# Attention and a gated feed-forward on one core: the second half of a pair's value product in three bursts instead of two

## The chip, the cores and the metric

The kernel runs on one NeuronCore of a Trainium2 chip. The metric is the device time of one execution in microseconds (us), as the median of several runs; lower is better. Engines are named as in the profile: PE (TensorE matmul), PEld (its weight loads), DVE (VectorE), ACT (ScalarE), POOL (GpSimd), and SP, which here only issues DMAs. Every engine takes its own instructions in the order in which they are written.

## What is computed

Input x is 4 batches of 1024 tokens with 128 channels. The reference, cut to what matters:

```
q, k, v = einsum('bsx,xMnd->Mbnsd', x, qkv)             # 16 heads of 64
a = q k^T * 64**-0.5 + bias                             # bias: cumulative by distance, -30000 above the diagonal
mix = softmax(a) v
x = layernorm(x + einsum('bnsd,ndx->bsx', mix, out_w))
xr, xk = blends of x and x shifted by one token         # by mu_r, mu_k
out = sigmoid(xr W_r) * (square(relu(xk W_k)) W_v)
x = layernorm(x + out)
```

## The kernel before, in words

The work goes in 32 pair steps, n = 0 to 31: 4 batches times 8 pairs of heads (`drive`, line 225). A pair has 16 rows of 128 queries; row r belongs to one head h and one query tile i (`ROWS`, line 26). Rows 0 to 7 are the query tiles 0 to 3 of both heads and rows 8 to 15 the tiles 4 to 7. A row of query tile i covers i + 1 key tiles (causal), so rows 0 to 7 are 1, 2, 3, 4, 1, 2, 3, 4 key tiles wide, and rows 8 to 15 are 5, 6, 7, 8, 5, 6, 7, 8.

A pair step has 16 slots, and every engine has its own loop over the slots (`step` on lines 343, 514, 704 and 998). What happens to a row runs across the engines: PE computes its scores four slots ahead (`score`, line 900; `LEAD` = 4), DVE adds the bias and takes the row's minimum (`bias`, line 605), ACT takes exp and the sum (`exps`, line 458), DVE takes the reciprocal of the sum (`invert`, line 620, issued one slot later, behind the next row's `bias`), POOL multiplies the row by it (`normalise`, line 406), PE transposes the row in slot r (`transpose`, line 921) into one of two PSUM banks in turn, four key tiles to a bank, and ACT or DVE copies each bank to SBUF (`evacuate`, lines 466 and 624; which engine, by the string `EVACUATOR`, line 63). A bank of `transpose` waits for the copy two banks earlier. In the text T(r) is the transpose of row r, S(r) its scores; S(16) is row 0 of the next pair. With the banks of rows 7, 8 and 9 it goes so: row 7 is one bank, copied by ACT; row 8 is two, the first copied by DVE and the second by ACT; row 9 is two, both by DVE. So T(9) waits for DVE's copy of row 8's first bank.

The transposed rows times v are the pair's mix (`mix`, line 934): for each key tile j and both heads one matmul, summed in the PSUM bank `ps_o`. The near half (g = 0, query tiles 0 to 3, key tiles 0 to 3) is done in slot 11 of the same step (`MIX_NEAR`). The far half (g = 1, query tiles 4 to 7, key tiles 0 to 7) can only start when row 15's transposes are copied, so it is done in the next step, in two bursts of four key tiles, in slots 2 and 5 (`MIX_FAR`, line 83; PE's `step`, lines 1006 to 1008). Key tiles 0 to 4 take 512 columns, 5 to 7 take 384, 256 and 128. Within a slot PE's order is: scores, projection chunk, tile step, far mix, near mix, transposes (lines 999 to 1011). When the last key tile is done, DVE copies `ps_o` to `mix_sb` (`store_mix`, line 635), the far half at the end of slot `MIX_FAR[1] + 1` = 6, the near half in slot 12.

Slots 2, 3, 5, 7, 10 and 14 also hold the six projection chunks of the next pair (`PROJ_SLOTS`, line 73; `project`, line 873): chunks 0 and 1 are q, 2 and 3 are k, 4 and 5 are v, all through the one PSUM bank `ps_m`. A q or k chunk is rounded by ACT (`q_hi`, `k_hi`, line 450) and its rest is taken by DVE (`q_lo`, `k_lo`, line 601); the next user of `ps_m` waits for that (`wait_chunk`, line 855). From step 9 on a step also carries one tile of 128 tokens of the feed-forward (`tile_step`, lines 951, 640 and 478), whose matmuls use `ps_m` too: the output projection in slot 0 (line 960), the transpose of the normalised tile X1 in slot 4 (line 965), two products in slot 9 and one in slot 12. Steps 1 to 8 have far bursts but no tile; step 31 has a tile but no chunks.

SP issues the DMAs in one order (lines 343 to 377): the tables and weights to come, after chunk 1 the four pieces of `stacks` from q, then `store_mix(n - 1, 1)` (line 363; it waits for DVE's copy of the far half), then after chunk 3 the eight pieces of `stacks` from k (line 279), then `x_res` and `mix_tile` for the next step's tile (lines 325 and 329), then `store_mix(n, 0)`. S(16) waits for the stacks of head 0, the output projection for `mix_tile`.

Of the kernel before, what the change touches and what calls it, by code (L numbers as in the profile page):

```python
# [15 lines left out]
GROUP = 4  # L16
# [49 lines left out]
def evacuated(engine, k):  # L66

    return sum(int(c) == engine for c in EVACUATOR[:k + 1])
# [11 lines left out]
V_PROJ, LN2_RSTD, LN2 = 12, 13, 13  # L80
TILE_MATMULS = (OUT_PROJ, X1_T, RK_PROJ, V_PROJ)
WIDE = 4
MIX_FAR = (2, 5)
MIX_NEAR = 11
TILE_LAG = PAIRS + 1
CH = 13
# [2 lines left out]
def build(nc, x, qkv, out_w, rpe, w_r, w_k, w_v, mu_r, mu_k, out):  # L89
# [13 lines left out]
    with ExitStack() as ctx:  # L103
# [149 lines left out]
        def rows_ahead(n, more, slot):  # L253

            if slot + LEAD < NROWS:
                return [(n, slot + LEAD)]
            return [(n + 1, slot + LEAD - NROWS)] if more else []
# [317 lines left out]
        def _(dve):  # L575
# [19 lines left out]
            def project(m, c):  # L595

                dve.wait_ge(s_hi, 4 * m + c + 1)
                which, at = chunk_of(m, c)
                hi, lo, scale = ((q_hi, q_lo, SCALE), (k_hi, k_lo, 1.0))[which]
                half = slice(512 * at, 512 * at + 512)  # L600
                nc.vector.scalar_tensor_tensor(out=lo[:, half], in0=proj_bank(m, c), scalar=scale,  # L601
                                               in1=hi[:, half].bitcast(F32), op0=ALU.mult, op1=ALU.subtract)\
                    .then_inc(s_lo, 1)

            def bias(n, r):

                h, i = ROWS[r]
                width = P * (i + 1)
                if i % GROUP == 0:
                    dve.wait_ge(s_table[n % 2][h], 16 * (n // 2) + 16)  # L610

                before = (r - PSLOTS) % NROWS
                dve.wait_ge(s_tr, NBANKS * (n if before > r else n + 1) + sum(b[0] <= before for b in BANKS))
                dve.wait_ge(s_score, NROWS * n + r + 1)
                nc.vector.tensor_tensor_reduce(prob[:, r % PSLOTS, 0:width],  # L615
                                               ps_rows[:, score_at(r):score_at(r) + width],
                                               table[n % 2][:, h, 0:width][:, ::-1], 1.0, 3.0e38, ALU.add, ALU.min,
                                               low[:, r:r + 1]).then_inc(s_biased, 1)

            def invert(n, r):  # L620
                dve.wait_ge(s_exp, NROWS * n + r + 1)
                nc.vector.reciprocal(inv[:, r:r + 1], total[:, r:r + 1]).then_inc(s_inv, 1)  # L622

            def evacuate(n, k):
                r, b0, nb = BANKS[k]
                h, i = ROWS[r]
                g = i // GROUP
                dve.wait_ge(s_pv, 2 * n + g + 1)
                if n == 0 and r == 3 * GROUP:
                    dve.wait_ge(s_xt_dram, 16 * (BATCH - 1))  # L630
                dve.wait_ge(s_tr, NBANKS * (n + 1) + k + 1)
                nc.vector.tensor_copy(pt[h][g][:, b0:b0 + nb, P * (i % GROUP):P * (i % GROUP) + P],  # L632
                                      ps_t[k % 2][:, 0:nb * P].rearrange("p (b s) -> p b s", s=P)).then_inc(s_ev[0], 1)

            def store_mix(n, g):
                dve.wait_ge(s_pv, 2 * n + g + 3)
                dve.wait_ge(s_mix_d[g], 16 * n + 16)
                nc.vector.tensor_copy(mix_sb[g][:, :], ps_o[:, :]).then_inc(s_o, 1)  # L638
# [65 lines left out]
            def step(n, prev, tile_too, more):  # L704
                for slot in range(NROWS):
                    for row in rows_ahead(n, more, slot):
                        bias(*row)
                    for row in rows_ahead(n, more, slot - 1):
                        invert(*row)
                    if more and slot in PROJ_SLOTS[:4]:  # L710
                        project(n + 1, PROJ_SLOTS.index(slot))
                    for k in range(NBANKS):
                        if BANKS[k][0] == slot and EVACUATOR[k] == "0":
                            evacuate(n, k)
                    if prev and slot == MIX_FAR[1] + 1:
                        store_mix(n - 1, 1)
                    if slot == MIX_NEAR + 1:
                        store_mix(n, 0)
                    if tile_too:
                        tile_step(n, slot)  # L720

            drive(step)

            def add_residual(w):
# [101 lines left out]
        def _(pe):  # L826
# [73 lines left out]
            def score(n, r):  # L900

                h, i = ROWS[r]
                if n == 0 and r == 0:
                    pe.wait_ge(s_first, 96)
                elif i % GROUP == 0:
                    pe.wait_ge(s_stack[h], 96 * n + 96)

                pe.wait_ge(s_biased, NROWS * n + r + 3 - rows_since(r))
                at, width = score_at(r), P * (i + 1)
                cut = BANK - at % BANK  # L910
                for c0, c1 in ((0, min(cut, width)), (cut, width)):
                    if c0 >= c1:
                        continue
                    c1 = max(c1, c0 + SHORTEST)
                    for low_part in range(2):
                        ins = nc.tensor.matmul(ps_rows[:, at + c0:at + c1], q_st(h, n)[:, P * i:P * i + P],  # L916
                                               k_st(h, n, low_part)[:, c0:c1], start=(low_part == 0),
                                               stop=(low_part == 1))
                ins.then_inc(s_score, 1)

            def transpose(n, r):
                pe.wait_ge(s_norm, NROWS * n + r + 1)
                for k in (k for k in range(NBANKS) if BANKS[k][0] == r):
                    _, b0, nb = BANKS[k]

                    engine = int(EVACUATOR[k - 2])
                    pe.wait_ge(s_ev[engine], EVACUATED[engine] * (n + (k >= 2)) + evacuated(engine, (k - 2) % NBANKS))
                    for b in range(nb):
                        at = P * (b0 + b)
                        ins = nc.tensor.transpose(ps_t[k % 2][:, P * b:P * b + P], prob[:, r % PSLOTS, at:at + P],  # L930
                                                  ident[:, :])
                    ins.then_inc(s_tr, 1)

            def mix(n, g, first, end):

                if first == 0:
                    pe.wait_ge(s_v, 2 * n + 2)
                    for which in range(2):
                        last_bank = max(k for k in range(NBANKS) if ROWS[BANKS[k][0]][1] < GROUP * (g + 1))
                        pe.wait_ge(s_ev[which], EVACUATED[which] * (n + 1) + evacuated(which, last_bank))  # L940
                    pe.wait_ge(s_o, 2 * n + g + 1)
                final = GROUP * (g + 1) - 1
                for j in range(first, end):
                    c0 = P * max(0, j - GROUP * g)
                    for h in range(2):
                        ins = nc.tensor.matmul(ps_o[D * h:D * h + D, c0:], v_pair[n % 2][:, j, D * h:D * h + D],  # L946
                                               pt[h][g][:, j, c0:], start=(j == 0), stop=(j == final))
                    if j == final:
                        ins.then_inc(s_pv, 1)
# [48 lines left out]
            def step(n, prev, tile_too, more):  # L998
                for slot in range(NROWS):
                    for row in rows_ahead(n, more, slot):  # L1000
                        score(*row)
                    if more and slot in PROJ_SLOTS:
                        project(n + 1, PROJ_SLOTS.index(slot), tile_too)
                    if tile_too:
                        tile_step(n, slot, more)
                    if prev and slot in MIX_FAR:
                        at = GROUP * MIX_FAR.index(slot)
                        mix(n - 1, 1, at, at + GROUP)
                    if slot == MIX_NEAR:
                        mix(n, 0, 0, GROUP)  # L1010
                    transpose(n, slot)

            drive(step)

            def out_project(w):
# [81 lines left out]
```

## Time and profile before

| what | value |
|---|---|
| median of 3 runs | 1245.46 us (1243.80, 1245.46, 1245.80) |
| the profiled execution's own time | 1246.39 us |
| its span, first to last instruction | 1244.6 us |
| mean granted TensorE clock | 0.988 of full speed |
| PE busy | 1118.1 us, 90% |
| POOL busy | 886.9 us, 71% |
| DVE busy | 843.3 us, 68% |
| ACT busy | 743.1 us, 60% |
| chain that ended last | PE 65%, DVE 17%, issue 8%, ACT 6% |

Busy shares are means over all stages. A row of a timeline is: start in us from the span's start, length, engine, line, operation, written tile <- read tiles, shape, number of instructions run together, and in brackets the engine's idle time before it and what ended that. The length of a PE row runs to a modelled end, so the distance between the starts of neighbours is the better measure of what a PE instruction costs. A matmul on fp32 data shows as two rows.

### The profile page before, as it was taken

What the parts mean: (1) busy time and instruction counts of PE and PEld (TensorE: products, weight loads), DVE (VectorE), ACT (ScalarE), POOL (GpSimd) and SP (SyncE); (2) the same over time, 40 slices, a digit from 0 to 9 for tenths busy, and PEclk for the clock granted to TensorE, in tenths of its full rate; (3) what the DMA queues carried; (4) which work ended last, traced back from release to release, by engine and by line L of the source; (5) the groups of instructions that cost most, each with busy time, mean ns of one, the idle gap of its engine ahead of it and who ended that gap; (6) DMA issues with size and microseconds to landing.
All of it is one profiled execution on the core that took longest, in us unless ns stands there. A gap on an engine that the chain in (4) does not pass through costs nothing.

```text
span 1244.6 us, 21976 instructions
## 1 busy us (share of the span) xinstructions
PE 1118.1 (90%) x6909; PEld 781.9 (63%) x6909; DVE 843.3 (68%) x2505; ACT 743.1 (60%) x1857; POOL 886.9 (71%) x527
## 2 busy tenths in 40 slices
PE   5899999999999999999999999999999999999885
PEld 3666666666666666666666666666666666666664
DVE  2666666666676767777667777666777676777746
ACT  3666666666655656656665656665656566656623
POOL 1877777878876677876677876677876677776730
PEclk9899999999999999999999999999999999999997
DMA  8855445555655455655465654456654455654600
GB/s 199 208 122 124 115 117 122 130 132 134 157 138 115 116 141 127 160 137 129 116 141 132 159 127 118 117 140 153 159 123 115 123 134 142 155 122 110 213 18 20
DMA packets 101745, 163.69 MB, mean 132 GB/s; under 512 B 10592, under 2 KB 66288, under 8 KB 101632
## 3 DMA queue, kind: packets, MB, share of 16 engines
q1 hardware_dynamic: 99472, 161.37, 53.4%
q10 hardware_dynamic: 2160, 0.92, 0.3%
q8 instruction: 58, 0.95, 0.3%
q14 instruction: 55, 0.45, 0.1%
HBM read 41.63 MB, written 19.96 MB: 49 GB/s over the span
## 4 chain that ended last, share of the span: by engine, by line
PE 65%; DVE 17%; issue 8%; ACT 6%; POOL 2%; DMA 1%; DVEq 0%; SPq 0%; ACTq 0%
PE ps_o L946 21%; PE ps_t L930 15%; PE ps_rows L916 13%; PE ps_m L891 7%; DVE prob L615 4%; DVE pt L632 4%; PE ps_m L960 4%; PE ps_m L896 3%; ACT pt L474 2%; DVE mix_sb L638 2%; POOL prob L410 2%; ACT prob L463 1%; DVE k_lo L601 1%; DVE q_lo L601 1%; DVE shift L682 1%
## 5 line engine op out<-in xcount | busy, mean ns | idle before, releaser
L410 POOL TENSOR_SCALAR prob<-prob,inv 128x128 f32<-128x128 f32 (+7 forms) x512 | 880.5, 1730 | 308.2 <-DVE inv L622 306.2
L463 ACT ACTIVATE prob<-prob,low 128x128 f32<-128x128 f32 (+7 forms) x512 | 395.3, 773 | 119.1 <-DVE low L615 116.9
L615 DVE CUSTOM_DVE_ANT_0 prob<-ps_rows,table 128x128 f32<-128x128 f32 (+7 forms) x512 | 383.6, 749 | 72.7 <-PE ps_rows L916 66.2
L930 PE MATMUL ps_t<-ident,prob 128*128 128x128 f32 x2304 | 349.1, 278 | 87.2 <-ACT pt L474 50.1
L916 PE MATMUL ps_rows<-stacks 128*128 128x512 f32 (+3 forms) x1536 | 402.5, 372 | 4.6 <-DVE w_t L700 3.2
L930 PEld LDWEIGHTS ps_t<-ident,prob 128*128 128x128 f32 x2304 | 260.6, 141 | 198.3 <-issue 130.6
L632 DVE COPY pt<-ps_t 128x256 f32<-128x256 f32 (+2 forms) x320 | 179.1, 568 | 179.6 <-PE ps_t L930 178.8
L474 ACT ACTIVATE pt<-ps_t 128x128 f32<-128x128 f32 (+2 forms) x448 | 203.6, 477 | 110.8 <-PE ps_t L930 110.6
L946 PE MATMUL ps_o<-pt,v_pair 128*64 128x512 f32 (+3 forms) x1536 | 268.7, 492 | 0.0
L916 PEld LDWEIGHTS ps_rows<-stacks 128*128 128x128 f32 x1536 | 246.3, 191 | 22.7 <-DVE w_t L700 3.4
L946 PEld LDWEIGHTS ps_o<-pt,v_pair 128*64 128x64 f32 x1536 | 101.8, 136 | 181.8 <-issue 172.3
L891 PE MATMUL ps_m<-x_cur,w_cur 128*128 128x512 f32 x250 | 130.6, 604 | 0.0
L622 DVE RECIPROCAL inv<-total 128x1 f32<-128x1 f32 x512 | 81.7, 160 | 71.6 <-ACT prob L463 70.0
L450 ACT ACTIVATE q_hi<-ps_m 128x512 fp32r<-128x512 f32 x63 | 37.2, 590 | 119.4 <-PE ps_m L891 119.4
L463 ACT ACTIVATION_READ_ACCUMULATOR prob<-prob,low 128x1 f32 x512 | 98.0, 191 | 0.0
L896 PE MATMUL ps_m<-w_cur,x_cur 128*128 128x128 f32 x504 | 66.4, 275 | 0.0
L896 PEld LDWEIGHTS ps_m<-w_cur,x_cur 128*128 128x128 f32 x504 | 65.1, 191 | 0.1
L601 DVE SCALAR_TENSOR_TENSOR q_lo<-ps_m,q_hi 128x512 fp32r<-128x512 f32 x63 | 43.6, 692 | 26.7 <-ACT q_hi L450 26.6
L455 ACT ACTIVATE v_pair<-ps_m 128x512 f32<-128x512 f32 x63 | 37.6, 597 | 28.1 <-PE ps_m L896 27.6
L484 ACT ACTIVATE lnv<-mv,eps 128x1 f32<-128x1 f32 x48 | 14.1, 295 | 65.3 <-DVE mv L653 36.9
L891 PEld LDWEIGHTS ps_m<-x_cur,w_cur 128*128 128x128 f32 x250 | 43.3, 191 | 11.7 <-issue 5.8
L960 PE MATMUL ps_m<-wo,mix_tile 128*128 128x128 f32 x384 | 47.8, 279 | 0.0
(108 smaller groups left out, 561.6 us busy)
## 6 DMA issues: line engine op xcount, KB each, us to landing
stacks<-k_hi SPq DMA_DIRECT2D x126, 256.0 KB, 4.7
stacks<-k_lo SPq DMA_DIRECT2D x126, 256.0 KB, 4.9
stacks<-q_hi SPq DMA_DIRECT2D x63, 256.0 KB, 3.7
stacks<-q_lo SPq DMA_DIRECT2D x63, 256.0 KB, 4.4
mix_transposed<-mix_sb SPq DMA_DIRECT2D x62, 256.0 KB, 2.0
table<-bias_by_distance SPq DMA_DIRECT2D x64, 192.0 KB, 3.7
mix_tile<-mix_transposed SPq DMA_DIRECT2D x24, 512.0 KB, 5.0
w_cur<-in_L_attn_qkv SPq DMA_DIRECT2D x31, 192.0 KB, 3.9
```

The source lines that it names most:

```text
L410: nc.gpsimd.tensor_scalar(row, row, inv[:, r:r + 1], None, ALU.mult).then_inc(s_norm, 1)
L463: nc.scalar.activation(row, row, ACT.Exp, bias=low[:, r:r + 1], scale=-1.0, accum_out=total[:, r:r + 1]).then_inc(s_exp, 1)
L474: nc.scalar.activation(pt[h][g][:, b0:b0 + nb, P * (i % GROUP):P * (i % GROUP) + P], ps_t[k % 2][:, 0:nb * P].rearrange("p (b s) -> p b s" ...
L615: nc.vector.tensor_tensor_reduce(prob[:, r % PSLOTS, 0:width], ps_rows[:, score_at(r):score_at(r) + width], table[n % 2][:, h, 0:width][:, ...
L622: nc.vector.reciprocal(inv[:, r:r + 1], total[:, r:r + 1]).then_inc(s_inv, 1)
L632: nc.vector.tensor_copy(pt[h][g][:, b0:b0 + nb, P * (i % GROUP):P * (i % GROUP) + P], ps_t[k % 2][:, 0:nb * P].rearrange("p (b s) -> p b s ...
L891: ins = nc.tensor.matmul(proj_bank(m, c), w_cur[m % 2][:, which, :], x_cur[:, 512 * at:512 * at + 512], start=True, stop=True)
L896: ins = nc.tensor.matmul(proj_bank(m, c)[:, P * t:P * t + P], x_cur[:, at:at + P], w_cur[m % 2][:, 2, :], start=True, stop=True)
L916: ins = nc.tensor.matmul(ps_rows[:, at + c0:at + c1], q_st(h, n)[:, P * i:P * i + P], k_st(h, n, low_part)[:, c0:c1], start=(low_part == 0 ...
L930: ins = nc.tensor.transpose(ps_t[k % 2][:, P * b:P * b + P], prob[:, r % PSLOTS, at:at + P], ident[:, :])
L946: ins = nc.tensor.matmul(ps_o[D * h:D * h + D, c0:], v_pair[n % 2][:, j, D * h:D * h + D], pt[h][g][:, j, c0:], start=(j == 0), stop=(j == ...
L960: ins = nc.tensor.matmul(ps_m[:, 0:C], mix_tile[:, p, :], wo[:, p, :], start=(p == 0), stop=(p == PAIRS - 1))
```

## The change

The far half is cut in three bursts in place of two: key tiles 0 and 1 in slot 1, 2 and 3 in slot 4, 4 to 7 in slot 7. DVE's copy of the finished half, and with it SP's store, moves from slot 6 to slot 8. No instruction is added or taken away.

```
-MIX_FAR = (2, 5)
+MIX_FAR = {1: (0, 2), 4: (2, 4), 7: (4, 8)}
...
-                    if prev and slot == MIX_FAR[1] + 1:
+                    if prev and slot == max(MIX_FAR) + 1:
                         store_mix(n - 1, 1)
...
                     if prev and slot in MIX_FAR:
-                        at = GROUP * MIX_FAR.index(slot)
-                        mix(n - 1, 1, at, at + GROUP)
+                        mix(n - 1, 1, *MIX_FAR[slot])
```

## Rows read from the trace of the kernel before

**Rows 1.** Busy time in one step with a tile: stretch, length, PE, PEld, DVE, ...

```profile
636.60:674.10 37.50, 34.48 (x216) 24.14 (x216) 26.72 (x81) 23.10 (x60) 27.61 (x17) 1.00 0.55 132
```

**Rows 2.** Timeline of PE, first half of that step, slots 2 to 9

```profile
640.56 1.10 PE L891 MATMUL ps_m<-x_cur,w_cur 128*128 128x512 f32 x2
641.59 3.65 PE L946 MATMUL ps_o<-pt,v_pair 128*64 128x512 f32 x16
645.17 0.55 PE L930 MATMUL ps_t<-ident,prob 128*128 128x128 f32 x3
...
646.03 1.02 PE L891 MATMUL ps_m<-x_cur,w_cur 128*128 128x512 f32 x2
...
648.46 0.33 PE L965 MATMUL ps_m<-ident,x 128*128 128x128 f32 x1 [0.39 <-DVE q_lo L601]
...
649.44 1.02 PE L891 MATMUL ps_m<-x_cur,w_cur 128*128 128x512 f32 x2
650.39 2.37 PE L946 MATMUL ps_o<-pt,v_pair 128*64 128x512 f32 x16
...
655.05 1.02 PE L891 MATMUL ps_m<-x_cur,w_cur 128*128 128x512 f32 x2
655.91 0.60 PE L930 MATMUL ps_t<-ident,prob 128*128 128x128 f32 x4
...
659.70 0.85 PE L930 MATMUL ps_t<-ident,prob 128*128 128x128 f32 x6 [0.76 <-DVE pt L632]
```

**Rows 3.** Timeline of DVE, same step, slots 6 to 9

```profile
655.65 0.68 DVE L638 COPY mix_sb<-ps_o 128x512 f32<-128x512 f32 x1
...
658.86 0.69 DVE L632 COPY pt<-ps_t 128x512 f32<-128x512 f32 x1
...
660.43 1.02 DVE L632 COPY pt<-ps_t 128x512 f32<-128x512 f32 x2
```

**Rows 4.** Timeline of PE, a step without a tile: T(7) and T(9)

```profile
216.37 0.60 PE L930 MATMUL ps_t<-ident,prob 128*128 128x128 f32 x4
...
220.16 0.85 PE L930 MATMUL ps_t<-ident,prob 128*128 128x128 f32 x6 [1.21 <-DVE pt L632]
```

**Rows 5.** Timeline of PE, second half of the first step, to the next step's slot 0

```profile
662.10 0.93 PE L930 MATMUL ps_t<-ident,prob 128*128 128x128 f32 x7
...
666.19 1.09 PE L930 MATMUL ps_t<-ident,prob 128*128 128x128 f32 x8
667.04 0.49 PE L916 MATMUL ps_rows<-stacks 128*128 128x256 f32 x2
...
669.73 0.85 PE L930 MATMUL ps_t<-ident,prob 128*128 128x128 f32 x6 [0.97 <-ACT pt L474]
...
672.51 0.96 PE L930 MATMUL ps_t<-ident,prob 128*128 128x128 f32 x7 [0.69 <-ACT pt L474]
...
675.23 0.94 PE L960 MATMUL ps_m<-wo,mix_tile 128*128 128x128 f32 x7
```

**Rows 6.** Timeline of DVE, same step: the reciprocal of row 15

```profile
669.13 0.16 DVE L622 RECIPROCAL inv<-total 128x1 f32<-128x1 f32 x1 [0.48 <-ACT prob L463]
```

**Rows 7.** Timeline of SP's DMA issues, same step

```profile
656.36 0.33 SPq L320 DMA_DIRECT2D mix_transposed<-mix_sb  x1
658.16 1.10 SPq L279 DMA_DIRECT2D stacks<-k_hi  x2
...
667.84 0.99 SPq L329 DMA_DIRECT2D mix_tile<-mix_transposed  x1
```

**Rows 8.** Line 279, 659.7 to 660.9 us: the two k_lo pieces of head 0

```profile
L279 SPq DMA_DIRECT2D stacks<-k_lo x2: 647/990/1333, 659.3 to 660.0; - x2
...
DMA to landing us min/median/max: 4.5/4.9/5.3
```

**Rows 9.** Line 329, all 24 loads of mix_tile, issue to landing

```profile
DMA to landing us min/median/max: 4.7/5.0/5.6
```

**Rows 10.** DMA traffic from 662 to 668 us

```profile
DMA packets 396, 1.31 MB, mean 219 GB/s; under 512 B 77, under 2 KB 77, under 8 KB 395
...
q1 hardware_dynamic: 395, 1.30, 100.2%
```

## Prediction

> **What bounds the kernel now.** I read the page's shares first (PE 90%), then one step by stretch, then PE's timeline of it, and only then the engines that PE waits for. In a step with a tile PE is busy for 34.48 of 37.5 us, POOL for 27.6, DVE for 26.7, ACT for 23.1, at a granted clock of 1.00 [rows 1]. So PE sets the step, and what can be won or lost is its idle time. The reader should look for the brackets. The timeline shows four: 0.39 us before X1 in slot 4, until DVE has q_lo of chunk 1; 0.76 before T(9), until DVE has copied row 8 [rows 2]; 0.97 before T(13) and 0.69 before T(14), both for ACT copies [rows 5]. A step without a tile has 1.21 before T(9) [rows 4]. The change touches what lies before the first two; the later ones only matter as room.
>
> The wait before T(9) is DVE's doing. DVE copies the far half at 655.65, 0.68 us long, ahead of the bias of rows 11 and 12, and so reaches row 8's copy at 658.86, although PE has finished T(7) near 656.5 [rows 2, 3].
>
> **What moves on PE.** No instruction is added, so PE's own work stays, but for the entry into a burst. A q or k chunk lasts 0.86 from start to next start ahead of transposes (655.05 to 655.91) and 1.03 or 0.95 ahead of a burst [rows 2]: an entry costs about 0.1 to 0.17. Two entries become three. I take +0.03 a step with a tile and +0.1 without, with 0 and 0.17 as ends.
>
> **Cover lost: chunk 0 to chunk 1.** Chunk 1 waits until ACT and DVE have read chunk 0 out of the one bank. The same wait with nothing long over it is chunk 1 to X1: 646.03 to 648.46, 2.43 us, 0.39 of it idle [rows 2]. Before, the burst of 3.58 us in slot 2 (641.59 to 645.17) hid it. Afterwards slot 2 has no burst. Between chunks 0 and 1 PE has the chunk (0.86) and T(2) with S(7) (645.17 to 646.03, 0.86), 1.72 us, so it idles 2.43 - 1.72 = 0.71 us, in every step with chunks. X1 keeps its 0.39, as the slot 4 burst is issued behind it. Chunk 2 also loses its burst, but between chunks 2 and 3 there are 655.05 - 649.44 = 5.61 us, less the burst's 2.30 and its entry 3.2, still above 2.43: nothing.
>
> **The wait before T(9) changes hands.** With the copy of the far half gone from slot 6 and PE's slots 5 and 6 free of a burst, DVE has row 11 biased early. But the last burst now lies in slot 7, ahead of T(7). ACT's copy of T(7) stands ahead of the exp of row 11 on ACT; DVE's reciprocal of row 11 waits for that exp and stands ahead of the copy of row 8; T(9) waits for that copy. The same sequence exists one half later: T(11) starts at 666.19, then ACT's copy, the exp of the 8-tile row 15, and the reciprocal starts at 669.13, 2.94 us [rows 5, 6]. T(7) is 0.49 shorter (0.60 against 1.09), so 2.45. Then some 0.1 to the copy, 0.69 for it, and 0.15 to PE (659.55 to 659.70) [rows 2, 3]: 3.38 us from the start of T(7) to T(9). PE's own work there is 659.70 - 0.76 - 655.91 = 3.03 with a tile and 220.16 - 1.21 - 216.37 = 2.58 without [rows 2, 4]. So it still idles 0.35 (before 0.76) or 0.80 (before 1.21): a gain of 0.41 in both.
>
> Balance of the first half: with a tile +0.71 - 0.41 + 0.03 = +0.33 us, without +0.71 - 0.41 + 0.1 = +0.40 us.
>
> **DVE behind it.** The copy of the far half (0.68) now follows row 8's copy and delays row 13's bias and the two copies for T(10). From 659.55 to 660.43 DVE needs 0.88, then 1.02 for both copies; with 0.33 of shift and 0.62 for the store they end near 662.4, the first near 662.0. T(10) comes at 662.10 + 0.33 = 662.43 and needs the second only four transposes later [rows 3, 5]. Cost nothing, with 0.2 to 0.3 to spare; if the cover is gone, up to 0.3. The near mix waits for the same copy, but only in slot 11. POOL has 10 us idle in the step [rows 1].
>
> **SP behind it.** The far store waits for the copy, and the eight k pieces, x_res and mix_tile are queued behind the store. T(9) is now near 660.03, the copy of row 8 ends 0.15 earlier, the far copy near 660.5; then the store's issue (0.33) and the k pieces near 660.85 in place of 658.16: the whole train is 2.7 us later [rows 2, 3, 7]. Two takers are behind it.
> - S(16): the fourth k piece is issued at 660.0 and lands 5.3 later, 665.3 [rows 8]; then at 668.0, and S(16) wants it at 667.04 + 0.33. PE waits some 0.7 there. But T(13) waits 0.97 for ACT and T(14) 0.69 [rows 5], which this eats: nothing, with 0.8 as the other end.
> - mix_tile: issued at 667.84, 5.0 to land, 672.84 [rows 7, 9]; then 675.55, and the output projection wants it at 675.23 + 0.33 = 675.56 [rows 5]. It just fails to be hidden. The store's 256 KB now go right ahead of the train, so I take 0.2 us, ends 0 and 0.8 (a landing of 5.6 [rows 9] and the store).
>
> The train drains at 219 GB/s with the queue 100% busy [rows 10], so a late start is a late end. The Trainium skill (DMA: Bandwidth & Descriptors, Where 436 GB/s comes from) says instead that copies between places in SBUF are bound by the fabric at 435 GB/s; by that, the train would make up the delay, mix_tile would cost nothing, and the sum would be the first rival's. The trace has half that rate for the very same copies, and the measurement decides.
>
> **Sum.** Steps 9 to 30: 22 x (0.33 + 0.2) = 11.7. Steps 1 to 8: 8 x 0.40 = 3.2. Step 31 has no chunks and so no new gap, and I count it as nothing, though it may win a little. Together +14.9 us on the profiled execution's 1246.39, or 1261.3; that execution is 0.93 above the median, so 1260.4 for the median. I say **1260**.
>
> **Rivals.**
> - The transfers are hidden after all: the store's 0.2 is absent, because the train drains faster than rows 10 or because S(16) moves the next step too. Then 22 x 0.33 + 3.2 = 10.5, 1256. For it: the two times meet within 0.01 us. Against: the queue is full. Still slower.
> - The stacks are late in earnest: S(16) waits 0.7 to 0.8 and the ACT gaps do not absorb it, as T(12) also feeds the copy that T(13) waits for. 30 x 0.75 = 22.5 on top, 1283. Against it: 1.66 us of room in two gaps.
> - The relief of DVE wins (faster). If row 11's exp is done before the last burst ends, or the burst ends so early that T(9) finds its copy ready, the wait before T(9) goes whole: 22 x (0.71 - 0.76 + 0.03) + 8 x (0.71 - 1.21 + 0.1) = -0.4 - 3.2, 1242. It decides where copy, exp and reciprocal after T(7) take less than PE's own 3.03 or 2.58 against my 3.38. Against it: ACT's order, in which row 7's copy stands first. If the chunk gap is also below 0.71, it is more.
> - Gains and costs cancel: the gap at chunk 1 is 0.4 and nothing is late: 1245.
>
> **How the numbers follow.** Some 0.2% (2.5 us) is about what a measurement of this kernel tells from no change. Forecast 0.56, transfers hidden 0.18, stacks late 0.07: slower 0.81. Cancelled, 0.09: same. DVE's relief 0.10: faster. The likeliest case by itself, with entries, landing and the 3.38 each at their ends, spans 1249 to 1271. The range reaches down to the cancelled case and leaves out the faster case's lower part and the late stacks: 1243 to 1271.
>
> **What would show it.** Right: an idle of about 0.7 before chunk 1 in slot 3, released by q_lo; T(9) still waiting for DVE's copy, 0.3 to 0.4 with a tile and 0.8 without, with DVE's reciprocal of row 11 waiting for ACT just before; SP's k pieces 2.7 us later in the step; the output projection at or just behind mix_tile's landing; a step with a tile of about 38.0 us. Wrong: no idle at chunk 1, no wait before T(9), or a long idle before S(16) with T(13) and T(14) waiting as before.

## The result, and the profile after

The changed kernel takes 1289.47 us, the median of 4 runs (1284.88 to 1293.26), against 1244.83 for the kernel before (the three runs of the table above and a fourth): a ratio of 1.0357, 95% interval 1.0322 to 1.0392. It is slower, as forecast, but by 44.6 us where the sum said 14.9, and the time lies above the range. The profiled execution took 1289.75 us, with a span of 1288.0 and a mean granted clock of 0.988, the same as before.

I read the step first. Below is the busy time of one step with a tile, from 1.16 us ahead of its output projection to the same point of the next, with the columns of [rows 1].

```profile
659.82:698.76 38.94, 35.25 (x221) 24.34 (x218) 27.28 (x83) 23.37 (x60) 27.72 (x16) 1.00 0.53 128
```

The step is 38.94 us in place of 37.5 [rows 1], at a full clock. From the first output projection (step 9) to that of step 31 there are 22 steps: 824.3 us before (338.0 to 1162.3), 857.1 after (349.5 to 1206.6), so **+1.49 us a step**, 32.8 us in all. The first of these output projections itself starts 11.5 us later than before, from the eight steps without a tile, one start of a batch and the first mix_tile. What follows the output projection of step 31 gives about 1 back.

PE's timeline of that step, which answers to [rows 2, 5]; a row is start, length, engine, line, operation, tiles, shape, and in brackets the idle time before it and its releaser.

```profile
660.98 2.02 PE L960 MATMUL ps_m<-wo,mix_tile 128*128 128x128 f32 x16 [0.47 <-DMA mix_tile<-mix_transposed]
...
663.28 1.94 PE L946 MATMUL ps_o<-pt,v_pair 128*64 128x512 f32 x8
665.15 0.44 PE L930 MATMUL ps_t<-ident,prob 128*128 128x128 f32 x2
...
665.78 1.02 PE L891 MATMUL ps_m<-x_cur,w_cur 128*128 128x512 f32 x2
...
668.29 1.13 PE L891 MATMUL ps_m<-x_cur,w_cur 128*128 128x512 f32 x2 [0.70 <-DVE q_lo L601]
...
670.83 0.33 PE L965 MATMUL ps_m<-ident,x 128*128 128x128 f32 x1 [0.39 <-DVE q_lo L601]
...
677.00 1.02 PE L891 MATMUL ps_m<-x_cur,w_cur 128*128 128x512 f32 x2
...
680.25 0.66 PE L930 MATMUL ps_t<-ident,prob 128*128 128x128 f32 x4
...
683.67 0.85 PE L930 MATMUL ps_t<-ident,prob 128*128 128x128 f32 x6 [0.48 <-DVE pt L632]
...
691.67 0.50 PE L916 MATMUL ps_rows<-stacks 128*128 128x256 f32 x2 [0.42 <-DMA stacks<-k_lo]
...
693.70 0.85 PE L930 MATMUL ps_t<-ident,prob 128*128 128x128 f32 x6 [0.52 <-ACT pt L474]
...
696.35 0.96 PE L930 MATMUL ps_t<-ident,prob 128*128 128x128 f32 x7 [0.56 <-ACT pt L474]
...
698.74 0.48 PE L916 MATMUL ps_rows<-stacks 128*128 128x256 f32 x2
699.92 0.79 PE L960 MATMUL ps_m<-wo,mix_tile 128*128 128x128 f32 x5 [0.69 <-DMA mix_tile<-mix_transposed]
```

Two brackets are new: 0.70 before chunk 1, and 0.69 before the output projection. A third, S(16), waits 0.42 for stacks, but T(13) waits 0.52 for ACT in place of 0.97 and T(14) 0.56 in place of 0.69 [rows 5], so in this step that wait only replaces others. T(9) waits 0.48 in place of 0.76 [rows 2].

A bracket counts from the modelled end of what ran before. The scores ahead of the output projection start 1.18 us before it (699.92 - 698.74); in the kernel before it is 0.32 (675.23 - 674.91), so from start to start the wait costs 0.86.

```profile
674.91 0.48 PE L916 MATMUL ps_rows<-stacks 128*128 128x256 f32 x2
```

S(16) does not wait so little everywhere. In a step without a tile, from T(9) to T(13):

```profile
82.57 0.85 PE L930 MATMUL ps_t<-ident,prob 128*128 128x128 f32 x6 [0.93 <-DVE pt L632]
...
91.71 0.50 PE L916 MATMUL ps_rows<-stacks 128*128 128x256 f32 x2 [1.55 <-DMA stacks<-k_lo]
...
93.49 0.84 PE L930 MATMUL ps_t<-ident,prob 128*128 128x128 f32 x6 [0.49 <-ACT pt L474]
```

T(9) to T(13) is 10.92 here, 10.56 in the next step and 10.98 in the last of the first batch (S(16) waits 1.55, 1.21 and 1.61); in the other steps with chunks it is 10.02 to 10.46, and before 10.02 to 10.05.

A step without a tile, T(9), which answers to [rows 4]:

```profile
224.92 0.85 PE L930 MATMUL ps_t<-ident,prob 128*128 128x128 f32 x6 [0.93 <-DVE pt L632]
```

The next T(9) starts at 260.17, 35.25 us later; before, 34.40 lie between (220.16 to 254.56). That is +0.85 a step.

Who holds T(9): DVE in the step with a tile [rows 3, 6].

```profile
682.76 0.16 DVE L622 RECIPROCAL inv<-total 128x1 f32<-128x1 f32 x1 [0.26 <-ACT prob L463]
682.84 0.69 DVE L632 COPY pt<-ps_t 128x512 f32<-128x512 f32 x1
683.45 0.68 DVE L638 COPY mix_sb<-ps_o 128x512 f32<-128x512 f32 x1
```

ACT copies T(7) at 681.00 and takes the exp of row 11 from 681.50 on; DVE's reciprocal waits for that, and the copy that T(9) wants stands behind it. The copy of the far half comes third, and SP waits for it [rows 7]:

```profile
684.15 0.33 SPq L320 DMA_DIRECT2D mix_transposed<-mix_sb  x1
684.52 1.10 SPq L279 DMA_DIRECT2D stacks<-k_hi  x2
...
694.10 1.14 SPq L329 DMA_DIRECT2D mix_tile<-mix_transposed  x1
695.28 0.81 SPq L320 DMA_DIRECT2D mix_transposed<-mix_sb  x1
```

The first k piece leaves 23.54 us after the output projection (684.52 - 660.98), before 20.39 (658.16 - 637.77); mix_tile 33.12 after it, before 30.07. The loads of mix_tile, issue to landing [rows 9], take longer as well:

```profile
DMA to landing us min/median/max: 4.7/5.6/6.0
```

The traffic from 688 to 694 us is [rows 10] again:

```profile
DMA packets 398, 1.31 MB, mean 218 GB/s; under 512 B 80, under 2 KB 80, under 8 KB 397
...
q1 hardware_dynamic: 397, 1.30, 100.1%
```

And PE's waits over the whole execution: us in total, times, the longest. The three have no row before, as PE waited for none of them in the steps.

```profile
PE ps_m L891 <- DVE q_lo L601: 21.5, 31, 0.7
...
PE ps_rows L916 <- DMA stacks<-k_lo: 18.1, 30, 1.6
PE ps_m L960 <- DMA mix_tile<-mix_transposed: 16.9, 23, 1.5
```

### The profile page after: what moved, and what is told of

It is laid out like the page before. It is cut to its first block, busy times and chain, and to the rows that moved or that the text cites. A ratio compares the mean times of both kernels' runs of the same rounds, so it can differ in the third digit from the quotient of the medians.

```text
span 1288.0 us, 21976 instructions
## 1 busy us (share of the span) xinstructions
PE 1134.9 (88%) x6909; PEld 782.6 (61%) x6909; DVE 851.3 (66%) x2505; ACT 749.7 (58%) x1857; POOL 890.2 (69%) x527
## 4 chain that ended last, share of the span: by engine, by line
PE 53%; DMA 14%; SPq 10%; ACT 8%; DVE 7%; issue 5%; POOL 2%; ACTq 0%; DVEq 0%
PE ps_o L946 17%; PE ps_rows L916 10%; DMA mix_tile<-mix_transposed 10%; PE ps_t L930 9%; PE ps_m L891 9%; SPq L279 8%; PE ps_m L960 4%; DMA stacks<-k_lo 3%; DVE q_lo L601 3%; ACT prob L463 3%; ACT pt L474 3%; ACT q_hi L450 3%; POOL prob L410 2%; PE ps_m L896 1%; DVE pt L632 1%
## 5 line engine op out<-in xcount | busy, mean ns | idle before, releaser
L930 PEld LDWEIGHTS ps_t<-ident,prob 128*128 128x128 f32 x2304 | 263.4, 141 | 201.0 <-issue 172.2
L946 PE MATMUL ps_o<-pt,v_pair 128*64 128x512 f32 (+3 forms) x1536 | 275.5, 494 | 0.5
L891 PE MATMUL ps_m<-x_cur,w_cur 128*128 128x512 f32 x250 | 132.7, 612 | 21.5 <-DVE q_lo L601 21.5
L960 PE MATMUL ps_m<-wo,mix_tile 128*128 128x128 f32 x384 | 48.8, 281 | 16.9 <-DMA mix_tile<-mix_transposed 16.9
L960 PEld LDWEIGHTS ps_m<-wo,mix_tile 128*128 128x128 f32 x384 | 45.1, 193 | 21.0 <-issue 21.0
```

The lines of the kernel that those rows point to most:

```text
L891: ins = nc.tensor.matmul(proj_bank(m, c), w_cur[m % 2][:, which, :], x_cur[:, 512 * at:512 * at + 512], start=True, stop=True)
L960: ins = nc.tensor.matmul(ps_m[:, 0:C], mix_tile[:, p, :], wo[:, p, :], start=(p == 0), stop=(p == PAIRS - 1))
```

## The experiments

The theory that these rows suggest: a step is a loop. PE's first half up to the last burst, DVE's copy of the far half, SP's store, the k pieces, mix_tile, and the next output projection follow one another, and this loop is longer than PE's own work. Three edits of the changed kernel take a suspect each away; I call them **A** (the store leaves the front of the train), **B** (chunk 0 gets its cover back) and **C** (T(7) goes ahead of the last burst).

**A, the far store behind the eight k pieces.**

```
-                if prev:
-                    store_mix(n - 1, 1)
                 if more:
                     sp.wait_ge(s_lo, 4 * n + 8)
                     for h in range(2):
                         stack_k(n + 1, h, s_stack[h])
+                if prev:
+                    store_mix(n - 1, 1)
```

> The changed kernel with one edit on SP: the store of the far half is issued behind the eight k pieces instead of ahead of them. Theory A (the changed kernel is the sum of several waits, one of them the DMA train that starts 2.7 us later because it is queued behind the store): the waits of the output projection for mix_tile (16.9 us of idle in 23 steps, some 0.8 a step from start to start) and of S(16) for the stacks (18.1 us) go; the second was hidden behind ACT copies and gives nothing, the first gives 22 x 0.8 = 18 us: about 1272. Rival B (mix_tile lands late because of what is queued right behind it, not because the train starts late): the wait for mix_tile stays, 1285 or more.

Measured: 1262.86 (ratio 1.0141, 1.0126 to 1.0157), 26.6 below the changed kernel and some 9 below what the theory gave. SP's issues in a step of it whose output projection starts at 685.85:

```profile
704.75 1.10 SPq L279 DMA_DIRECT2D stacks<-k_hi  x2
...
712.99 1.26 SPq L320 DMA_DIRECT2D mix_transposed<-mix_sb  x1
...
715.97 0.61 SPq L329 DMA_DIRECT2D mix_tile<-mix_transposed  x1
```

The k pieces leave 18.90 us after the output projection, not 23.54, mix_tile 30.12, not 33.12, and PE's list of waits names neither stacks nor mix_tile. Every one of the 22 steps is 38.01 to 38.04 long, which is PE's own path with the three bursts: 0.56 above before. The other 0.93 of the 1.49 is the train. Of the 9 us that the theory lacks, 22 x 0.13 = 2.9 are that a step gains 0.93 and not 0.8; 5.9 lie ahead of the first output projection, which starts at 343.6 and not 349.5: with the train on time S(16) does not wait in the steps without a tile either.

**B, the first burst back in slot 2.**

```
-MIX_FAR = {1: (0, 2), 4: (2, 4), 7: (4, 8)}
+MIX_FAR = {2: (0, 2), 4: (2, 4), 7: (4, 8)}
```

> The changed kernel with its first burst (key tiles 0 and 1) in slot 2 instead of slot 1, behind chunk 0. Theory A (the lost cover of chunk 0 costs 0.80 us a step from start to start and 0.1 more for the restart): the idle of 0.70 before chunk 1 goes in 30 steps, 24 to 27 us less: about 1264. Rival C (three entries into a burst and the short bursts are what costs, the chunk wait only moves): under 8 us less, 1281 or more.

Measured: 1264.35 (1.0145, 1.0123 to 1.0167), as expected. The wait before chunk 1 is gone from PE's list of waits (21.5 us before the edit); mix_tile is still late, 13.5 us in 19 steps. So the missing cover of chunk 0 is worth 25.1 us.

**C, the last burst behind T(7)** in the same slot.

```
-                    if prev and slot in MIX_FAR:
+                    if prev and slot in MIX_FAR and slot != max(MIX_FAR):
                         mix(n - 1, 1, *MIX_FAR[slot])
...
                     transpose(n, slot)
+                    if prev and slot == max(MIX_FAR):
+                        mix(n - 1, 1, *MIX_FAR[slot])
```

> The changed kernel with the last burst issued behind T(7) in slot 7 instead of ahead of it. Theory A (T(9) waits for a chain that starts at T(7): ACT's copy, row 11's exp, its reciprocal, row 8's copy): T(7) is 2.3 us earlier, the chain ends before PE is there, the idle before T(9) (0.48 with a tile, 0.93 without) goes: 22 x 0.48 + 8 x 0.93 = 18 us less, about 1271. Rival E (the wait before T(9) is set by row 12's bias or by the copy of row 8 itself, both behind the burst): no change, 1285 or more.

Measured: 1283.88 (1.0304, 1.0283 to 1.0324), only 5.6 less, where the theory had 18. In the steps with a tile T(9) waits no more, yet the step falls only from 38.96 to 38.63. The k pieces leave 23.21 us after the output projection in place of 23.54: the step falls by what the train gains.

**All combinations.** A and B, A and C, B and C, and all three, so that each edit is seen on each ground.

> The changed kernel with two edits at once: SP's far store behind the eight k pieces (alone -26.6 us of the median, 1262.9) and the first burst back in slot 2 (alone -25.1, 1264.4). Theory A, two loops set a step and the longer one wins: with the store behind the k pieces the loop of copy, store, k pieces and mix_tile is out of the way and PE's own path sets the step; the first burst in slot 2 then takes the 0.7 to 0.8 us idle before chunk 1 out of 30 steps, 21 to 24 us: 1239 to 1242. Rival C, PE's later waits for ACT take up what the chunk gives back: 1250 or more. Rival D, both edits only shorten the same loop: no better than the better one, 1260 to 1264.

> The changed kernel with SP's far store behind the eight k pieces (alone 1262.9) and the last burst issued behind T(7) (alone only -5.6, 1283.9). Theory A: PE's path sets the step once the loop through SP is loosened, so the edit on PE now shows its whole worth, the 0.48 us idle before T(9) in 22 steps and 0.93 in 8, 18 us: 1244 to 1250. Rival D, effects simply add (-26.6 - 5.6): 1257. Rival C, the copy of the far half ends later behind the later burst and DVE delays T(10): 1262 or more.

> The changed kernel with the first burst back in slot 2 (alone 1264.4) and the last burst issued behind T(7) (alone 1283.9), the far store still ahead of the k pieces. Theory A: the loop through DVE's copy, the store, the k pieces and mix_tile still sets the step, and the later burst does not bring the copy sooner, so little comes on top: 1256 to 1264. Rival B, the loop was only at its limit because chunk 1 was late, so now PE's path sets the step: 18 us on top, 1244 to 1249.

> The changed kernel with three edits at once: first burst in slot 2, last burst behind T(7), far store behind the k pieces. Theory A (the sum of waits): no chunk wait but X1's, no wait before T(9), no late train; PE sets the step, 0.76 and 1.21 less idle than before for 0.1 to 0.3 more in entries: 1222 to 1234, faster than before. Rival F (once these waits are gone the next one takes their place, DVE's copies for T(10) or POOL's rows): 1240 or more.

The step is the mean of the 22 distances of output projections; the wait is PE's for mix_tile, in total (times).

| edits | median us | ratio to before, 95% interval | step us | wait for mix_tile |
|---|---|---|---|---|
| none (the change) | 1289.47 | 1.0357, 1.0322 to 1.0392 | 38.96 | 16.9 (23) |
| A | 1262.86 | 1.0141, 1.0126 to 1.0157 | 38.03 | none |
| B | 1264.35 | 1.0145, 1.0123 to 1.0167 | 38.14 | 13.5 (19) |
| C | 1283.88 | 1.0304, 1.0283 to 1.0324 | 38.63 | 14.0 (22) |
| A, B | 1236.67 | 0.9941, 0.9924 to 0.9958 | 37.25 | 0.3 (1) |
| A, C | 1253.67 | 1.0078, 1.0063 to 1.0093 | 37.72 | none |
| B, C | 1255.09 | 1.0091, 1.0073 to 1.0110 | 37.85 | 13.8 (21) |
| A, B, C | **1227.59** | **0.9876, 0.9860 to 0.9893** | 36.93 | none |

The kernel before, timed again beside each group of runs, had medians of 1243.4 to 1244.9, so a difference of 1 or 2 us between groups says nothing. Of the four expectations the theory's range held for A, B, C; A, B came 2 below its range, B, C 1 below, and A, C 4 above, near the plain sum of the single effects.

Three things follow. First, the effects add, nearly: A gives 26.6, 27.7, 30.2 and 27.5 us, B 25.1, 26.2, 28.8 and 26.1, C 5.6, 9.3, 9.2 and 9.1. (C alone gives less: its first output projection starts 1.1 later than that of the change, 350.6 against 349.5. S(16) waits 1.2 to 1.6 us in six of the eight steps before it, and in three of them the clock falls, as in the last section.) A and B together give 52.8 us (1289.47 - 1236.67), more than the 44.6 lost: without these two costs the change is a gain of 0.6%. Second, my picture of two separate loops of which the longer one wins is wrong: then neither A nor B alone could have won 25 us. The step with the store in front is 0.89 to 0.93 above the one without, whatever PE's path is (38.96 - 38.03, 38.14 - 37.25, 38.63 - 37.72, 37.85 - 36.93). PE's first half is the common part of both paths; only behind the copy do they part, and there the train is 0.9 longer than PE's own second half. The k pieces say the same: in the four kernels with the store in front (none, B, C, and B with C) the first leaves 23.54, 22.75, 23.21 and 22.42 us after the output projection, and the step is 15.4 longer each time. Third, the kernel with all three edits beats both kernels, by 1.2% and 4.8%.

C on top of A does not give the whole idle time. T(9) in a step without a tile, with A and C:

```profile
219.26 0.85 PE L930 MATMUL ps_t<-ident,prob 128*128 128x128 f32 x6 [0.57 <-DVE pt L632]
```

0.93 has become 0.57, and the step with a tile 38.03 has become 37.72, 0.31 for an idle time of 0.49. 30 x 0.3 is the 9 us measured, half of the 18 that I had expected for A and C together.

**Is it DVE that wins by the late copy?** The bursts of before, in slots 2 and 5, but DVE's copy (and so SP's store) only at the end of slot 8; then the same with the store behind the k pieces.

```
-MIX_FAR = {1: (0, 2), 4: (2, 4), 7: (4, 8)}
+MIX_FAR = {2: (0, 4), 5: (4, 8)}
...
-                    if prev and slot == max(MIX_FAR) + 1:
+                    if prev and slot == 8:
```

> The kernel of before with its two bursts (slots 2 and 5), and only DVE's copy of the far half moved from slot 6 to slot 8. Theory A: DVE's relief alone is a gain; the wait before T(9) falls from 0.76 to about 0.1 with a tile and from 1.21 to about 0.5 without; the k pieces start some 2 us later in the step, which mix_tile's slack of 2.4 covers but for 0 to 0.3 a step: 1224 to 1233. Rival D (the late copy is what hurts, by the train and by the copies queued behind it on DVE): 1250 or more.

> The kernel of before with DVE's copy of the far half in slot 8 (as in the run of two bursts with the late copy) and, besides, SP's far store behind the k pieces. Theory A (the late copy's own price of 16 us there was the DMA train queued behind it): the waits of the output projection and of S(16) go, and with T(9) released 0.1 to 0.2 earlier the time is that of before or a little less, 1238 to 1248. Rival D (the late copy also costs by what it delays on DVE): 1253 or more.

Measured: 1261.25 (1.0140, 1.0109 to 1.0171) and 1246.23 (1.0017, 1.0001 to 1.0033). My theory missed the first by 28 us: a late copy costs 16 us by itself (beside it the kernel before took 1244.89), and all but some 3 of them go with the order on SP (beside that run 1243.51), so they are the train's; there the theory's 1238 to 1248 held. In that run PE still waits for mix_tile 3 times, 3.1 us, each time at the first tile of a batch. It also shows where the relief of DVE went. PE's timeline, T(9) and T(14):

```profile
696.00 0.84 PE L930 MATMUL ps_t<-ident,prob 128*128 128x128 f32 x6 [0.55 <-DVE pt L632]
...
709.07 0.95 PE L930 MATMUL ps_t<-ident,prob 128*128 128x128 f32 x7 [0.96 <-ACT pt L474]
```

T(9) waits 0.55 in place of 0.76 [rows 2] and T(14) 0.96 in place of 0.69 [rows 5]: 0.21 won, 0.27 given back five slots later. Most of its steps are 37.43 to 37.46, where before has 37.47.

**What the third burst costs by itself.** Three bursts in slots 2, 3 and 5, the copy in slot 6 as before.

```
-MIX_FAR = {1: (0, 2), 4: (2, 4), 7: (4, 8)}
+MIX_FAR = {2: (0, 2), 3: (2, 4), 5: (4, 8)}
```

> Three bursts that keep the old places and the old copy: key tiles 0 and 1 in slot 2, 2 and 3 in slot 3 (behind chunk 1), 4 to 7 in slot 5, copy in slot 6. Every chunk wait is covered, the train starts as before, so this weighs the third entry alone against the 0.39 before X1 that the burst in slot 3 now covers. Theory A (an entry costs 0.1 to 0.25): X1's 0.39 goes in 22 steps, 31 entries more: 1238 to 1244. Rival C (three short bursts are what makes the change slow): 1252 or more.

Measured: 1249.68 (1.0055, 1.0037 to 1.0072), between the two expectations. PE waits for no DMA in its steps, so this is PE's own price. One of the two short bursts, and what follows it:

```profile
642.47 1.94 PE L946 MATMUL ps_o<-pt,v_pair 128*64 128x512 f32 x8
644.34 0.55 PE L930 MATMUL ps_t<-ident,prob 128*128 128x128 f32 x3
```

A short burst lasts 1.87 from start to next start, two of them 3.74; the long one lasted 3.58 [rows 2]. A step without a tile is 34.69 (80.40 to 115.09, two T(9)) in place of 34.40: **0.29 for one more burst**. With a tile the step is 37.60, +0.13, since the burst in slot 3 also covers X1's old wait of 0.39; another of 0.2 comes before chunk 2, for ACT's copy of X1.

**Is mix_tile slow because of what is issued behind it?** The changed kernel, with the near store behind the tile's output.

```
-                store_mix(n, 0) if more else None
...
                 if tile_too:
                     tile_store(n - TILE_LAG)
+                store_mix(n, 0) if more else None
```

> The changed kernel with SP's near store issued behind the store of the finished tile, so some 1.5 us later and no longer right behind mix_tile; the train ahead of mix_tile is untouched. Rival B (mix_tile takes 5.6 in place of 5.0 us to land because transfers issued right behind it share the engines): its landing falls to about 5.0, the output projection's wait by 0.6 a step, about 1276. Theory A (mix_tile is late because of the train ahead of it alone): landing and time stay, 1286 or more.

Measured: 1282.80 (1.0321, 1.0301 to 1.0342), 6.7 less, between the two. The loads of mix_tile:

```profile
DMA to landing us min/median/max: 4.7/5.1/6.5
```

The median goes from 5.6 to 5.1, the mean step from 38.96 to 38.58 ((1199.9 - 351.2) / 22), and PE's wait for mix_tile from 16.9 us to 9.2. So 0.5 of the 0.6 by which it lands later came from the store that is issued 1.2 us behind the load; before, 2.1 us lay between them (667.84 [rows 7] to 669.93).

**Is the store's place worth something in the kernel before too?**

Here the edit on SP of A, with the bursts in slots 2 and 5 and the copy in slot 6:

```
-MIX_FAR = {1: (0, 2), 4: (2, 4), 7: (4, 8)}
+MIX_FAR = {2: (0, 4), 5: (4, 8)}
...
-                if prev:
-                    store_mix(n - 1, 1)
                 if more:
...
+                if prev:
+                    store_mix(n - 1, 1)
```

> The kernel before with one edit, SP's far store behind the eight k pieces. Theory A: in the kernel before the copy of the far half is 2.7 us sooner and nothing on PE waits for stacks or mix_tile, so the order on SP is worth nothing: 1242 to 1247. Rival B, the store costs the train something before as well: 1235 to 1240.

Measured: 1254.31 (1.0080, 1.0065 to 1.0095). Both theories missed: the edit that wins 27 us in the changed kernel loses 10.9 here. SP's issues at the start of a batch, in a step whose output projection should start at 640.4:

```profile
631.55 1.30 SPq L320 DMA_DIRECT2D mix_transposed<-mix_sb  x1
632.89 1.61 SPq L325 DMA_DIRECT2D x_res<-in_L_attn_x  x1
637.45 0.37 SPq L329 DMA_DIRECT2D mix_tile<-mix_transposed  x1
```

The first tile of a batch needs this very store, and SP holds the load until it has landed: 3 such waits, 7.3 us on SP, the longest 2.9; the step comes 1.5 us late. In an ordinary step the store costs the train too. Before, it went out in a gap of the queue, 1.8 us ahead of the k pieces [rows 7]; now it stands in the full train, and mix_tile leaves 31.61 us after the output projection (673.55 - 641.94) in place of 30.07. PE waits for mix_tile 6 times, 6.2 us, and the other steps are up to 0.3 longer; what makes up those 0.3 stays open.

Why it wins in the changed kernel: there chunk 3 comes earlier, 16.02 us after the output projection (677.00 - 660.98) in place of 17.28 (655.05 - 637.77), because only two short bursts stand ahead of it and not both long ones. In the kernel with all three edits the k pieces leave 18.10 us after the output projection (684.11 - 666.01), in the kernel before 20.39. The change has 2.3 us of train to give away, but its store, waiting for slot 8, holds them.

## Why the prediction was wrong

The direction and the mechanisms came as forecast, but three prices of the sum were too small: that of mix_tile above all, that of the entries into a burst, and that of S(16), which was put at nothing.

- **Chunk 0 to chunk 1.** Forecast 0.71 idle; measured 0.70, released by q_lo, in the steps with chunks. Right. From c0 to c1 2.51 lie, 0.79 more than PE's own 1.72, and c1 itself lasts 0.10 longer behind the wait (668.29 to 669.25, 0.96 against 0.86), which the sum lacks.
- **The wait before T(9).** The chain over ACT's copy, the exp and the reciprocal of row 11 is the one forecast, and as long: 3.42 us from T(7) to T(9) (680.25 to 683.67) against 3.38. But PE's own work behind a burst is 2.94, not 3.03, so it idles 0.48 and 0.93 against 0.35 and 0.80: 0.28 won, not 0.41.
- **The entry into a burst.** Here a step of the sum failed. I priced a third burst by the chunk ahead of it alone, +0.03 with a tile and +0.1 without, with 0.17 as the end. It costs 0.29 without a tile (the run of three bursts with the old copy), as two short bursts also last 0.16 longer than a long one, and 0.16 with a tile (next point).
- **Balance of the first half.** Forecast +0.33 and +0.40. Output projection to T(9) is 22.69 after and 21.93 before (683.67 - 660.98, 659.70 - 637.77): +0.76, of which 0.70 + 0.10 is the chunk, -0.28 T(9), 0.08 the slower start behind the late mix_tile, and the last 0.16 the entries. Without a tile +0.85.
- **S(16).** Forecast: some 0.7 of wait that the gaps before T(13) and T(14) eat. It waits 0.42 with a tile (0.68 without, at 197.94), and T(9) to T(13) is 10.03 both before and after (659.70 to 669.73, 683.67 to 693.70). Right in most steps, but not in three without a tile: there the wait is 1.2 to 1.6, and T(9) to T(13) is 0.89, 0.53 and 0.95 longer, 2.4 us that the sum puts at nothing. As a cost of every step the rival of stacks late in earnest is out; the time came near its 1283 for another reason.
- **mix_tile.** This is **the step that failed most**: I took 0.2 us, with 0.8 as the end, and A removes 0.93. The train starts 3.15 later, not 2.7, as the first half is longer; mix_tile leaves 3.05 later and lands in 5.6, not 5.0. Of the 3.65 the 2.39 of room before (675.23 - 672.84) and PE's 0.56 cover 2.95, so 0.70 is left, near the bracket of 0.69. From start to start that wait is 0.86, and with the slow restart (0.08) it makes up the 0.93. I had PE's path and the train meet within 0.01 us, and there each error of a term before the copy counts in full: the slack was a difference of two sums, and I gave it a bound as if it were one price.
- **The relief of DVE.** Its rival said that the wait before T(9) would go; it didn't. Even where the copy is late and T(9) waits less, T(14) takes it back.
- **The sum.** Forecast 22 x 0.53 + 8 x 0.40 = 14.9. Measured 22 x 1.49 = 32.8, and 11.5 before the first tile: 8 x 0.85 = 6.8, less 0.9 by which step 0, which the change does not touch, came sooner (T(9) at 47.32, before 48.20), 2.4 for S(16) in three steps, 1.6 for the low clock in the last of them (below), and 1.6 for the first mix_tile, for which PE waits 1.52. Step 31 did not win: 33.56 from its output projection to the last one, before 33.43. What lies behind that is 1.0 shorter (47.8, before 48.9).

The queue is 100.1% busy at 218 GB/s, so the late start stayed a late end, as [rows 10] said; the 435 GB/s of the Trainium skill (DMA: Bandwidth & Descriptors, Where 436 GB/s comes from) is not reached by these copies in any run: in 5 us of the k pieces of one step each run moves 216 to 220 GB/s.

## What to carry to other kernels

When a change moves the instruction that a DMA queue waits for, write the loop that runs over that queue as a sum beside the engine's own, and where the two meet within a few tenths, add every error of the common part to the price instead of taking the meeting point. A store that another transfer's queue waits for is best placed where its data is ready before its turn: moved behind the k pieces it won 27 us where its data came late, and lost 11 where its data came early. A burst that is split costs at each new edge, and a burst that covered a wait should be moved only when something else covers it: the change with the store and the cover put right is 0.6% faster than the kernel before, and with T(7) ahead of the last burst as well 1.2%.

## What was not expected of the hardware

A wait has a cost behind its end. A pair of chunk matmuls lasts 0.96 from start to next start behind 0.70 of idle time and 0.86 without; the output projection to T(0) 1.86 behind a wait (660.98 to 662.84) and 1.78 without (637.77 to 639.55 in the kernel before).

One long wait was followed by a lower clock, another was not. At the start of the second batch S(16) waits 1.61 us for stacks (it starts at 269.37). Columns as in [rows 1]; the clock is the last but two.

```profile
268.00:270.00 2.00, 0.63 (x5) 0.64 (x6) 0.12 (x1) 1.57 (x3) 0.90 (x1) 1.00 1.00 223
270.00:272.00 2.00, 1.51 (x12) 1.33 (x11) 1.47 (x7) 1.14 (x4) 1.49 (x1) 0.87 0.96 205
272.00:274.00 2.00, 2.00 (x10) 2.00 (x9) 0.64 (x3) 1.36 (x4) 2.00 (x3) 0.50 0.42 141
```

PE was busy for 0.63 of 2 us, and from 272 to 274 us the granted clock is 0.50, the lower of the two levels, 1.2 GHz. The distance of the two T(9) around it is 37.80 (260.17 to 297.97) in place of 35.25: 0.95 of it before T(13), which is the wait, and 1.6 behind, where the clock is low. With A that step is 35.26 (258.43 to 293.69). The wait of 1.55 us before 91.71 left the clock as it was:

```profile
90.00:92.00 2.00, 0.45 (x4) 0.29 (x3) 0.52 (x1) 1.72 (x3) 1.30 (x1) 1.00 1.06 258
92.00:94.00 2.00, 1.51 (x14) 1.33 (x14) 1.38 (x7) 1.14 (x4) 1.14 (x1) 1.00 1.00 213
```

Here PE was busy for even less, 0.45 of 2 us. What sets the two apart, these rows do not show.

DVE's addition of two SBUF tiles (line 682) lasts 634 ns in the median before, 513 after and 868 with the bursts of before and the late copy, 291 at its shortest; its neighbour on line 681, of the same size but with one operand from PSUM, lasts 0.28 us in all three. POOL is at work beside it in the steps, but not at the shortest (at 1228.52 in the kernel before, between POOL instructions that end at 1226.5 and start at 1232.7). The Trainium skill (SBUF — State Buffer, SBUF: two separate sides) says that a DVE instruction with two inputs in SBUF and a POOL instruction that reads SBUF exclude each other from a shared port for a whole instruction. The trace agrees only in part: beside POOL the addition is 0.2 to 0.6 us longer, but it does not wait until POOL is done. In the changed kernel one runs from 655.38 to 655.89, inside a POOL instruction from 654.64 to 657.48 (spans on POOL are rough). In the kernels before and after no engine is shown waiting for this addition.
